# Attention's first group ahead of q's first chunk, and GpSimd's copy of q in four parts

## The reference

```python
q = relu((x @ Wq).reshape(b, s, 64, 64)) * SCALE
k = relu((x @ Wk).reshape(b, s, 64, 64))
v = (x @ Wv).reshape(b, s, 64, 64)
kv = einsum('bsid,bsjd->bsdj', k, v)
out = einsum('bsid,bsdj->bsij', q, kv)
q_norm = einsum('bsid,bsd->bsi', q, k.sum(axis=2))
out = (out / (q_norm[..., None] + EPS)).reshape(b, s, 64 * 64) @ Wo + bo
x = layernorm(x + out)
# fp4: blocks of 16 are scaled by max|x|/6, rounded to the FP4 grid and scaled back
h = silu(fp4(x) @ fp4(w_gate).T) * (fp4(x) @ fp4(w_up).T)
x = layernorm(x + fp4(h) @ fp4(w_down).T)
```

## Time and profile before

| | before |
|---|---|
| median of 3 runs | 2271.65 us (2270.31 to 2274.07) |
| the profiled execution | 2271.46 us, its span 2269.7 us |
| PE busy | 2050.3 us, 90% of the span |
| DVE busy | 1805.8 us, 80% |
| POOL busy | 1690.7 us, 74% |
| ACT busy | 1618.7 us, 71% |
| granted clock of TensorE | 0.985 of full speed |
| chain that ended last | PE 55%, POOL 18%, issue 9%, ACT 9%, DVE 6%, DMA 2% |

### The profile page before, as it was taken

The page is one execution under the profiler, slowest core; times in us unless marked ns, Lnnn a source line. Parts: engine busy times, 40 slices in busy tenths (PEclk is TensorE's granted clock), DMA queues, the critical chain, the costliest instruction groups (busy, mean ns, idle before and its releaser), DMA issues.

```text
span 2269.7 us, 88816 instructions
## 1 busy us (share of the span) xinstructions
PE 2050.3 (90%) x37963; PEld 1961.0 (86%) x37963; DVE 1805.8 (80%) x3359; ACT 1618.7 (71%) x3210; POOL 1690.7 (74%) x2192
## 2 busy tenths in 40 slices
PE   4799999999999999999999999999999999999975
PEld 3788998898898898898899899899899889889874
DVE  6778888888888888888888887888888888888873
ACT  4667777777777777777777777777777777777761
POOL 4577787787787787787787778778778778778772
PEclk9999999999999999999999999999999999999996
DMA  6467656666656666756756766765765665665661
GB/s 194 95 133 151 139 127 146 141 130 142 148 125 139 147 132 134 156 126 133 159 124 134 153 132 129 155 133 127 152 137 127 148 141 127 143 146 126 139 130 33
DMA packets 523216, 308.32 MB, mean 136 GB/s; under 512 B 275590, under 2 KB 497734, under 8 KB 522310
## 3 DMA queue, kind: packets, MB, share of 16 engines
q1 hardware_dynamic: 522822, 302.65, 61.9%
HBM read 17.38 MB, written 4.19 MB: 10 GB/s over the span
## 4 chain that ended last, share of the span: by engine, by line
PE 55%; POOL 18%; issue 9%; ACT 9%; DVE 6%; DMA 2%; SPq 0%; DVEq 0%; ACTq 0%; POOLq 0%
PE ps L408 15%; PE ps L361 12%; PE ps L363 12%; PE ps L362 12%; POOL o_st L1078 8%; POOL q_nat L1068 7%; ACT q_bd L564 6%; DVE q L798 3%; PE ps L434 3%; DVE o L816 2%; ACT hqT L571 2%; POOL small L1086 2%; PE ps L445 1%; DMA x_in<-in_L_attn_x 1%; ACT ks L577 1%
## 5 line engine op out<-in xcount | busy, mean ns | idle before, releaser
L1078 POOL TENSOR_TENSOR o_st<-o,o_st 128x256 bf16<-128x256 f32 x1024 | 659.8, 679 | 5.9 <-ACT o_st L639 5.9
L1068 POOL TENSOR_TENSOR q_nat<-q,q_nat 128x512 bf16<-128x512 f32 x512 | 590.3, 1176 | 33.2 <-ACT q_nat L597 32.9
L639 ACT CAST o_st<-o 128x256 bf16<-128x256 f32 x1024 | 358.4, 403 | 214.8 <-DVE o L816 211.0
L361 PE MATMUL ps<-v_st,q_bd 128*128 128x66 bf16 x4096 | 456.3, 198 | 42.9 <-DVE o L816 37.5
L361 PEld LDWEIGHTS ps<-v_st,q_bd 128*128 128x128 bf16 x4096 | 419.7, 114 | 61.9 <-DVE o L816 56.3
L362 PE MATMUL ps<-v_st,q_bd 128*128 128x66 bf16 x4096 | 454.0, 198 | 0.0
L363 PE MATMUL ps<-v_st,q_bd 128*128 128x66 bf16 x4096 | 452.5, 197 | 0.0
L816 DVE TENSOR_TENSOR o<-ps,rec 128x512 f32<-128x512 f32 x512 | 344.5, 683 | 120.7 <-POOL o_st L1078 110.2
L362 PEld LDWEIGHTS ps<-v_st,q_bd 128*128 128x128 bf16 x4096 | 417.5, 116 | 0.2 <-issue 0.2
L363 PEld LDWEIGHTS ps<-v_st,q_bd 128*128 128x128 bf16 x4096 | 416.8, 115 | 0.0
L408 PE MATMUL ps<-w_o,o_st 128*128 128x128 bf16 x6144 | 376.9, 220 | 3.4 <-DMA o_st<-swap 3.4
(11 more groups left out here) (129 smaller groups left out, 5334.4 us busy)
## 6 DMA issues: line engine op xcount, KB each, us to landing
q_bd<-q_nat SPq DMA_DIRECT2D x256, 256.0 KB, 3.9
swap<-v_st SPq DMA_DIRECT2D x64, 576.0 KB, 5.1
v_st<-v_st SPq DMA_DIRECT2D x64, 576.0 KB, 5.6
v_st<-swap SPq DMA_DIRECT2D x64, 576.0 KB, 5.4
swap<-o_st SPq DMA_DIRECT2D x64, 512.0 KB, 4.9
o_st<-o_st SPq DMA_DIRECT2D x64, 512.0 KB, 6.8
o_st<-swap SPq DMA_DIRECT2D x64, 512.0 KB, 5.5
x_in<-in_L_attn_x SPq DMA_DIRECT2D x64, 64.0 KB, 5.3
```

The costliest lines, as they stand in the source:

```text
L361: nc.tensor.matmul(dst, lhs(0), rhs(0), start=True, stop=False)
L639: last = nc.scalar.copy(ost[1 - t.par][:, 0, :, a, g * G:(g + 1) * G, :], src[:, a])
L1068: last = nc.gpsimd.tensor_tensor(qnat[:, 1, a, :, e, :], src[:, a], qnat[:, 0, a, :, e, :], ALU.subtract)
L1078: last = nc.gpsimd.tensor_tensor(lo[:, :, a], src[:, a], hi[:, :, a], ALU.subtract)
```

## The change

- TensorE: `h_transpose` stands ahead of k's chunk 2 instead of behind it, and `out_group(t, 0)` ahead of q's chunk 0.
- ScalarE: one copy of q (high part, upper half) moves from the middle of a turn to the end of the turn before (`q_stay_next`, ahead of `o_hi` 6 and 7). `x1_keep` moves ahead of `k_sums`, `o_hi` of group 0 ahead of `norm_o` of group 1 and `xq_copy`.
- VectorE: the small steps for x are spread otherwise between the `k_add`s; `scale_o` of group 0 and `residual_2` come ahead of `q_scale` 0; `recip` pairs are split into single ones; `h_scale` moves behind `scale_o` 2, `h_grid` behind `scale_o` 7.
- GpSimd: `q_stay` no longer waits for `x_one`, only for `rstd_1` or `h_back`, and is issued as four instructions (`STAYS`); `o_lo` 0 moves ahead of `q_lo` 0, and `rstd_2` and `x_bias` between `q_lo` 0 and `o_lo` 1.
- SyncE: the load `x_res` moves up from behind `x_in` to between the first moves of v and the second of o.

The slots and `USES` stay as they are. The core of the diff:

```diff
@@ SyncE
                     move(v4[t.par], vsw, s_vswap, vm[0], 0)
                 if t.mid:
+                    if t.back:
+                        sp.wait_ge(s_r1, t.b + 1)
+                    sp.dma_start(x_res[:, :], x_t[bass.ts(t.m, T), :]).then_inc(s_xres, 16)
+                if t.mid:
                     move(o4[t.par], osw, s_oswap, om[1], 1)
@@ TensorE
                 project(t, "k", 1)
+                h_transpose(t)
                 project(t, "k", 2)
-                h_transpose(t)
                 project(t, "k", 3)
...
                 down(t)
+                out_group(t, 0)
                 project(t, "q", 0)
-                out_group(t, 0)
                 k_sum(t)
@@ ScalarE
                 q_stay(t, 1, 0)
-                q_stay(t, 0, 1)
                 hq_copy(t)
                 q_stay(t, 0, 0)
                 norm_o(t, 0)
+                x1_keep(t)
                 k_sums(t)
...
-                x1_keep(t)
+                o_hi(t, 0)
                 norm_o(t, 1)
                 xq_copy(t)
                 q_hi(t, 0)
                 sigmoid(t)
-                o_hi(t, 0)
...
                 norm_o(t, 7)
+                q_stay_next(t)
                 o_hi(t, 6)
                 o_hi(t, 7)
@@ GpSimd, q_stay
-                if t.back:
-                    pool.wait_ge(s_x1, t.b + 1)
                 if t.end:
                     pool.wait_ge(s_hq, t.e + 1)
-                held = qnat[64:128, 1, 1].rearrange("p k e s -> p k (e s)")
-                nc.gpsimd.tensor_tensor(qbd[64:128, 1, :, 1, HALF:DH, :].rearrange("p k e s -> p k (e s)"),
-                                        held, consts[64:128, 4:5].unsqueeze(2).to_broadcast([64, NK, HALF * SB]),
-                                        ALU.mult).then_inc(s_qstay_p, 1)
+                elif t.back:
+                    pool.wait_ge(s_rs1, t.b + 1)
+                for k in range(0, NK, NK // STAYS):
+                    held = qnat[64:128, 1, 1, k:k + NK // STAYS].rearrange("p k e s -> p k (e s)")
+                    last = nc.gpsimd.tensor_tensor(
+                        qbd[64:128, 1, k:k + NK // STAYS, 1, HALF:DH, :].rearrange("p k e s -> p k (e s)"), held,
+                        consts[64:128, 4:5].unsqueeze(2).to_broadcast([64, NK // STAYS, HALF * SB]), ALU.mult)
+                last.then_inc(s_qstay_p, 1)
```

More of the change, by code:

```diff
@@ L57 @@
 OR = 2
+STAYS = 4
 EB = 4
@@ L317, in iteration @@
                     sp.dma_start(x_in[:, :], x_t[bass.ts(t.n + 2, T), :]).then_inc(s_x, 16)
-                if t.mid:
-                    if t.back:
-                        sp.wait_ge(s_r1, t.b + 1)
-                    sp.dma_start(x_res[:, :], x_t[bass.ts(t.m, T), :]).then_inc(s_xres, 16)
                 if t.front:
@@ L565, in q_stay @@
                                qnat[rows, l, a].rearrange("p k e s -> p k (e s)")).then_inc(s_qstay, 1)
+            def q_stay_next(t):
+                if not t.front:
+                    return
+                if t.attend:
+                    act.wait_ge(s_done["out"], (t.o + 1) * NG)
+                else:
+                    act.wait_ge(s_clear, 2)
+                act.wait_ge(s_qhi, (t.n + 1) * NC)
+                nc.scalar.copy(qbd[64:128, 0, :, 1, HALF:DH, :].rearrange("p k e s -> p k (e s)"),
+                               qnat[64:128, 0, 1].rearrange("p k e s -> p k (e s)")).then_inc(s_qstay, 1)
             def hq_copy(t):
@@ L980, in iteration @@
                 v_lo(t, 3)
+                x_max(t)
                 k_add(t, 1)
-                x_max(t)
+                x_scale(t)
                 k_add(t, 2)
+                x_recip(t)
                 x_lo(t)
-                x_scale(t)
+                x_norm(t)
                 k_add(t, 3)
-                x_recip(t)
-                x_norm(t)
-                residual_2(t)
                 x_top(t)
@@ L997, in iteration @@
                 recip(t, 0, 1)
+                scale_o(t, 0)
+                residual_2(t)
+                q_scale(t, 0)
                 stats_2(t)
-                q_scale(t, 0)
+                recip(t, 1, 1)
+                scale_o(t, 1)
                 before_mean_2(t)
                 mean_2(t)
-                recip(t, 1, 1)
-                scale_o(t, 0)
-                scale_o(t, 1)
                 gate_sig(t)
@@ L1008, in iteration @@
                 h_max(t)
+                recip(t, 2, 1)
+                scale_o(t, 2)
                 h_scale(t)
-                recip(t, 2, 2)
-                scale_o(t, 2)
+                recip(t, 3, 1)
                 scale_o(t, 3)
@@ L1021, in iteration @@
                 h_round(t)
-                recip(t, 6, 2)
+                recip(t, 6, 1)
                 scale_o(t, 6)
+                recip(t, 7, 1)
+                scale_o(t, 7)
                 h_grid(t)
-                scale_o(t, 7)
                 if t.is_(0):
@@ L1141, in iteration @@
                 x_back(t)
+                o_lo(t, 0)
+                q_lo(t, 0)
                 rstd_2(t)
-                q_lo(t, 0)
-                o_lo(t, 0)
+                x_bias(t)
                 o_lo(t, 1)
@@ L1148, in iteration @@
                 o_lo(t, 3)
-                x_bias(t)
                 q_lo(t, 2)
```

## The result

The changed kernel takes 2257.1 us (2255.39 to 2258.91), the one before 2272.19 beside it: 0.9933 of its time, 95% interval 0.9920 to 0.9945. 2264 was predicted, 2250 to 2282 as the range, with a chance of 0.5 for faster.

The account below looks back on a forecast made before the run. A repeating loop through TensorE, VectorE's folds, ScalarE, GpSimd and group 5 bounds the kernel. Per turn -0.68+0.61, taken as -0.11: -6.6 us over 60 turns, -1 for turn 64, from 2271.46 to 2264; range 2250 to 2282.

Parts of the forecast that it names:

- The loop: One turn, 33.75 us: TensorE's v and k, VectorE's folds, `q_scale` 0, `q_hi` 0, GpSimd's low parts, `scale_o` 3, group 5.
- First half: Turn up to the end of VectorE's folds: GpSimd's copy ends at 10.1, folds at 14.73, 0.68 us sooner.
- Second half: From the folds' end to group 5, through `q_scale` 0 and GpSimd's low parts: 0.61 us later per turn.
- the edges: Turns outside the 60 full ones: 1 us saved for turn 64, nothing counted for turns 0 to 3.
- the faster rival: GpSimd's copy without fixed cost per part, no push by `x_one`: -0.2 us a turn, 2258, down to 2250; chance 0.15.
- Rival, the lock: VectorE's `x_scale` shut out by GpSimd's copy until 10.46: +0.3 us a turn, 2289, half of it 2278; chance 0.15.
- Rival, the seam: Between turns, `q_stay_next` delays `v_hi` 0 and v's chunk 3 by 0.2 us: 2278 to 2284; chance 0.1.
- Costed at nothing: Earlier `x_res` load, o's last move, `o_hi` 0 ahead of `xq_copy`, ScalarE's copy at turn end: no time charged.

Follow-up runs that it names:

- e1: Changed kernel with q's chunk 0 ahead of group 0 on TensorE again: 2256.94 us, ratio 0.9928.
- e11: Changed kernel with `h_transpose` behind k's chunk 2 again: 2256.57 us, ratio 0.9933.
- e3: Changed kernel with `x_bias` back behind `o_lo` 3 on GpSimd: 2240.87 us, ratio 0.9861.
- e8: Changed kernel with `x_bias` behind `o_lo` 3, `rstd_2` ahead of `q_lo` 0 and `mean_2` ahead of `scale_o` 1: 2216.73 us, ratio 0.9765.
- e9: e8's kernel with `x_bias` between `x_back` and `o_lo` 0 on GpSimd: 2204.8 us, ratio 0.9703.
- e6: Changed kernel with `x_scale` behind `k_add` 2 on VectorE: 2264.4 us, ratio 0.9973.
- e4: Changed kernel with GpSimd's copy of q as one instruction (STAYS = 1), not waiting for `x_one`: 2479.4 us, ratio 1.0907.
- e5: Changed kernel with GpSimd's copy of q as one instruction that waits for `x_one` as before: 2287.2 us, ratio 1.0074.
- e7: Changed kernel with the load of `x_res` back behind `x_in` on SyncE: 2411.53 us, ratio 1.0622.
- e2: Changed kernel with ScalarE's copy of q's high upper half back in the middle of the turn: 2393.43 us, ratio 1.0533.
- e10: Kernel before the change with only group 0 moved ahead of q's chunk 0 on TensorE: 2371.24 us, ratio 1.0436.

## Why the prediction was right, point by point

- **The loop.** Right: group 5 waits for `scale_o` 3 and that for GpSimd, and the stall ahead of the down projection went and was not won. e1 and e11 show that TensorE's order is worth nothing beside the other moves, e3, e8 and e9 that GpSimd's run up to group 5 is where the turn is decided. The list of TensorE's stalls was incomplete: it had 1.08 and 0.17 and left out the 0.52 and the 0.36 shown above. The sum along the loop used neither. The moves on VectorE other than `x_scale`'s, `residual_2`'s and `scale_o` 0's above all, and `o_lo` 0's on GpSimd were not taken back one by one; what each is worth isn't shown.
- **First half.** -0.68 was said and -0.71 came (15.41 to 14.70), from two misses that cancel. The copy ended at 10.21 instead of 10.1 (it began at 6.12, not 5.95, with 0.17 us of idle time behind `h_back`, and took 4.09, not 4.0), so `k_add` 2 began at 10.15 instead of 10.08. The three small steps took 0.46 and not 0.55, with no idle time between them. `v_lo` 3 behind `x_one` came 0.56 late and not 0.4 (7.22 instead of 6.66), so the idle time ahead of `k_add` 1 did not hide it: `k_add` 1 began at 8.55 instead of 8.35, which cost nothing only because `k_add` 2 is held until 10.15.
- **Second half.** Said: 3.74 us to `q_lo` 0 and 5.20 on to `q_lo` 1, +0.61 together. Measured: 3.67 and 5.28, +0.62. `scale_o` 3 then stood 0.07 behind `q_lo` 1 instead of 0.15, which I had not counted. The turn: -0.11 said, -0.137 came, 1.6 us over 60 turns.
- **The term that was mis-sized: the edges.** I gave turn 64 one microsecond and turns 0 to 3 nothing; together they gave 3.3+1.8 = 5.1, so 4.1 us were missing here and 1.5 in the turns (8.1 where 6.6 was said). That is what the profiled execution shows: 2258.28, down by 13.2 where 7.6 was said; the median is another 1.2 under it. I had costed full turns alone. Part of the 3.3 can be chance: 1.25 of it is there already at `k_first` of turn 1 (74.89 before, 73.64 after), and among e1, e3, e6 and e11, which differ from the changed kernel only later, that row starts anywhere from 72.71 to 74.63. The other 2.0 came between turns 1 and 4, and there those four runs take 95.2 to 95.6 us as the changed kernel does (95.6), against 97.6 before. The end, too, is 100.4 to 101.7 us in those four, 102.2 in the changed kernel and 104.0 before: its gain is real, its size uncertain. In turn 2 group 0 waits for ScalarE's copy, so there the copy's move is on the path. Before:

```profile
113.64 0.22 PE L361 MATMUL ps<-v_st,q_bd 128*128 128x66 bf16 x1 [1.38 <-ACT q_bd L564]
```

After:

```profile
110.17 0.22 PE L362 MATMUL ps<-v_st,q_bd 128*128 128x66 bf16 x1 [0.68 <-ACT q_bd L565]
```

  In turn 1 this wait fell from 1.05 to 0.23, in turn 3 from 1.38 to 0.32. But a shorter wait is not a shorter turn: from `k_first` to `k_first` turns 1, 2 and 3 are 0.18, 1.35 and 0.50 shorter. Which other waits took the difference up or added to it, and where the gain at the end comes from, stays open.
- **The number, partly by luck.** 2257.1 is nearest to the 2258 of the faster rival, but not by its mechanism: that wanted a copy that ends by 9.8 and -0.2 us a turn, and the copy ended at 10.21 and a turn fell by 0.137. The forecast stood for a gain in the loop; of the 13.2 us the turns gave 8.1 and the edges, costed at one, gave 5.1.
- **Rival, the lock.** Its mechanism is real, and it decides: without the four parts the change is a loss (e4, e5). With them the copy ended at 10.21, just past the 10.15 from which the rival counts, and e6 puts the lock's cost at 0.08 us a turn. (Half of its 18 us would have given 2280, not 2278.) The Trainium skill (SBUF — State Buffer, Who interferes with whom) says that a `tensor_scalar` in a two-port mode contends with GpSimd and that the second of the two to issue is blocked until the first is done; the traces agree, for an instruction of 8 columns too (1.13 us in e5, 0.16 in e6 behind the copy's end). Whether `x_one` pushed the copy's second part, as the page's first-to-issue clause would have it, stays open: the fixed cost of a part and a push aren't separated in the 4.09.
- **Rival, the seam.** In the full turn after, `v_hi` 0 is some 0.15 us late and v's chunk 3 doesn't wait; the wait first appears when GpSimd's order is mended (0.08 in e3).
- **Costed at nothing.** The load of `x_res` was in time, and e7 shows what its cover is worth: some 155 us.

## What to carry to other kernels

Before an order is changed, find the loop that a turn repeats, and count an edit only where it stands on it: here the headline move was worth nothing, and `x_bias` (0.41) and part of `rstd_2` (1.26) moved into idle time of the same engine, with `mean_2`, were worth 0.88 us a turn, against 0.14 for the whole change. Where a large instruction on GpSimd runs beside steps of VectorE in SBUF that it shuts out, as here, it is cut into parts, so that they wait for a quarter of it. Cost the first and last turns by themselves, as other waits end last there.

## What the runs showed of the hardware

- TensorE's granted clock fell to 0.50, that is 1.2 GHz, behind short waits in a kernel whose TensorE is busy for some 90% of the time. In one such stretch of each of e2, e4, e5, e7 and e10, taken in windows of 0.1 us, it stayed there for 3.4 us. It came behind waits of 1.02 and 0.99 us (e2), 1.08 and 0.99 (e10), 0.66 and 0.62 (e5), one of 2.46 (e4) and one of 2.97 (e7). Chunk 0 took 2.54 instead of 1.34 us (e2), two chunks of k 4.32 instead of 2.68 (e4), the 42 matmuls of the output projection 4.11 instead of 2.52 (e7, e3): 1.2 to 1.6 us on top of the waits.
- The same waits don't bring it in every turn: it came in nearly each turn in e4, in each second in e2, in each third in e10 and in each fourth or fifth in e5. No stretch of 10 us between 170 and 2130 us has less than 1.00 in the kernel before, with its 1.08, in the changed one (0.28, 0.62 and 0.98) or in e1 (0.55, 0.62 and 0.99). What decides between e1's waits and e5's isn't shown. So a kernel of like turns can have turns of two lengths.
- A further part of a GpSimd copy cost at most (4.09-3.60)/3 = 0.16 us, a push by `x_one` included.
- An instruction of VectorE that is shut out gets in between two parts of the copy: `x_one` took 0.90 us beside parts of 1.02, and 3.52 beside the whole.
